# Transformer layers: the inverse roots of the query and key norms on another engine

## The chip, the cores and the metric

The kernel runs on one core of one Trainium2 chip. A core has five engines with a queue each: TensorE (PE in the profile), VectorE (DVE), ScalarE (ACT), GpSimd (POOL) and SyncE (SP), which issues most of the DMA transfers. The metric is the device time of one execution in microseconds, the median over the runs; lower is better.

## The reference

Two blocks run one after the other on x of shape (4, 512, 128). In the first, an attention that learns at test time is followed by a transformer of six layers. The second block has an attention with relative positions and a layer of experts. The change lies in the transformer of the first block. What matters of it, for each layer:

```python
def l2norm(t):
    return t / jnp.maximum(jnp.linalg.norm(t, axis=-1, keepdims=True), 1e-12)

def attn_layer(x, Wqkv, qs, ksc, Wo):
    ...
    q, k, v = (sh(q), sh(k), sh(v))          # 16 heads of 64
    q = l2norm(q) * qs
    k = l2norm(k) * ksc
    ...                                      # rotary, with cos, sin and a scale
    out = local_attention(q, k, v)           # windows of 32, each query sees its own and the one before
    return out.transpose(0, 2, 1, 3).reshape(b, n, INNER) @ Wo

for i in range(DEPTH):                       # 6 layers
    x = attn_layer(shift_tokens(x), Wqkv[i], q_scale[i], k_scale[i], Wo[i]) + x
    x = ffn_layer(shift_tokens(x), ln_g[i], ln_b[i], W1[i], b1[i], W2[i], b2[i]) + x
```

So each layer needs, for 4 batches, 512 tokens and 16 heads, the inverse root of a sum of 64 squares, once for queries and once for keys.

## The kernel before

The kernel has four phases with a meeting of all engines between them; the transformer is the second, from about 120 to 1850 us of the span. Its work is cut into 24 units, one for each layer and batch (unit u is layer u // 4, batch u % 4). A unit is laid over 110 steps ("rounds"), and a new unit starts every 32 steps, so up to four units overlap. No planner sorts the work: every engine walks through the same generator `rounds()` and issues, in each round, first the attention parts and then the units' steps that are due. Constants such as `NORM_AT` and `PART_AT` say at which step each piece of work is issued. A queue is in order, and the engines keep in step by semaphores alone; a `Signal` is one with named events.

The steps of one unit that matter here:

- Steps 0 to 31, eight times four steps: TensorE projects one group of four heads (lines 1109 to 1111, first four times keys, then four times queries), ScalarE squares it (line 1290), VectorE multiplies it with the rotary tables (line 1418, four instructions; it needs the tables' results of the group before to be merged), GpSimd adds the squares of the two halves (line 1552) and merges the rotated halves (lines 1558 and 1559). TensorE sums the squares over the head (line 1139), and VectorE collects the sums in `norms[kind]`, 128 x 128 numbers for one kind (lines 1427 and 1429; kind 0 is keys, kind 1 is queries). TensorE may project into a PSUM bank again only when VectorE has rotated what is in it.
- Step 17 ("root0", the key root) and step 33 ("root1", the query root): VectorE bounds `norms` from below (line 1434) and runs `inverse_root`, eleven instructions with a wait for the one before in front of each.
- The key roots then go through a DMA to memory and back, spread over partitions (lines 937 and 955), and VectorE multiplies the keys with them (line 1443). The query roots are transposed at step 39 (line 1143), copied by ScalarE (line 1295) and multiplied into the scores by VectorE (line 1485).

The attention of a unit is cut into eight parts of ten steps that start every four steps. For a part, TensorE computes scores (line 1208), VectorE scales them and takes the negated largest (lines 1485 and 1490), ScalarE takes exponentials with their sums (line 1354), VectorE inverts the sums (line 1493), GpSimd scales the exponentials (line 1573), TensorE transposes them (line 1216), ScalarE copies them (line 1360), TensorE weighs the values (line 1226), and after every second part mixes the heads (line 1234). The root steps fall one round before the round in which VectorE inverts the sums and GpSimd scales, of whichever part is due. The sync engine also issues the copies of the values into windows (lines 970 to 975), in the same order of rounds.

Of the kernel before, what the change touches and what calls it, by code (L numbers as in the profile page):

```python
# [10 lines left out]
I32 = mybir.dt.int32  # L11
ALU = mybir.AluOpType
# [4 lines left out]
P = 128  # L17
# [700 lines left out]
NORM_AT = {"root0": 17, "out": 15, "root1": 33, "turn": 39, "copy": 39}  # L718
# [67 lines left out]
def transformer_setup(c, t, scope):  # L786
# [8 lines left out]
    t.wide = [sb(f"rnorm_wide{i}", [P, S]) for i in range(2)]  # L795
    t.norms, t.rn, t.rn_t = [sb(f"norms{i}", [P, P]) for i in range(2)], [sb(f"rnorm{i}", [P, P]) for i in range(2)], t.wide[0][:, 0:P]
    t.rn_dram = [nc.dram_tensor(f"rnorms{i}", (32, S), F32, kind="Internal").ap() for i in range(2)]
    t.least, t.root_c = sb("least", [P, 1]), sb("root_constants", [P, 2], I32)
    t.rq = [sb(f"rnorm_tok{i}", [P, TPB, 32]) for i in range(2)]
    t.vt = [sb(f"v_tok{i}", [P, 2, PAIRS, DH]) for i in range(2)]  # L800
    t.v = [sb(f"v_win{i}", [P, TPB, PAIRS, DH]) for i in range(2)]
# [7 lines left out]
    one = lambda name, over: Signal(nc, "tf_" + name, over)  # L809
    pairs, halves = range(2 * GROUPS_TF), range(2)  # L810
    t.projected, t.squared, t.rotated = (per(n, units, [(p, h) for p in pairs for h in halves]) for n in ("projected", "squared", "rotated"))
    t.made, t.squares, t.summed, t.counted = (per(n, units, pairs) for n in ("made", "squares", "summed", "counted"))
    t.rooted, t.rn_turned, t.rn_kept = per("rooted", units, halves), one("rn_turned", units), one("rn_kept", units)
    t.rn_out = Signal(nc, "tf_rn_out", units, 16)
    t.wide_in = [Signal(nc, f"tf_wide_in{i}", [(u, g, j) for u in units for g in range(i, GROUPS_TF, 2) for j in range(4)], 16) for i in range(2)]
    t.k_scaled = per("k_scaled", units, range(GROUPS_TF))
# [584 lines left out]
def unit_vector(c, t, u, s):  # L1401
# [19 lines left out]
    if 0 <= p < 2 * GROUPS_TF and at == 0:  # L1421
        ps = ring_bank(c, t, "unit", u, f"sum{p}")[:, 0:P]
        kind, first = divmod(p, GROUPS_TF)
        V.wait_ge(*t.summed.on((u, p)))
        if first:
            V.wait_ge(*t.counted.on((u, p - 1)))
            V.e.tensor_tensor(t.norms[kind][:, :], t.norms[kind][:, :], ps, ALU.add).then_inc(*t.counted.by((u, p)))
        else:
            V.e.tensor_copy(t.norms[kind][:, :], ps).then_inc(*t.counted.by((u, p)))
    for kind in range(2):  # L1430
        if s == NORM_AT[f"root{kind}"]:
            x = t.norms[kind][:, :]
            V.wait_ge(*t.counted.on((u, GROUPS_TF * (kind + 1) - 1)))
            V.e.tensor_tensor(x, x, t.least[:, 0:1].to_broadcast([P, P]), ALU.max).then_inc(*own.up())
            if u:
                V.wait_ge(*(t.rn_turned if kind else t.rn_out).on(u - 1))
            inverse_root(c, t.rn[kind][:, :], x, t.rn_t, t.rooted.by((u, kind)), t.root_c)
    if s in SCALE_AT:
        g = SCALE_AT.index(s)
        k = t.k[u % 2][:, g, :, WIN:WIN + S]  # L1440
# [72 lines left out]
def transformer_pool(c, t):  # L1513
    G = c.G
    for high, low in t.xs:
        G.e.memset(high[:, :].bitcast(F32), 0.0)
        G.e.memset(low[:, :].bitcast(F32), 0.0)
    for k in t.k:
        G.e.memset(k[:, :, :, 0:WIN], 0.0)
    G.e.memset(t.v[0][:, 0, :, :], 0.0)  # L1520
    G.e.memset(t.xf[:, :], 0.0)
    G.e.memset(t.least[:, :], 1e-24)
    G.e.memset(t.root_c[:, 0:1], 1)
    G.e.memset(t.root_c[:, 1:2], 0x5F3759DF).then_inc(*t.zeroed.by(0))
    G.wait_ge(*t.normed.on(0))
    shift_gpsimd(c, t, 0)
    for now in rounds():
        for kind, n, s in now:
            if kind == "part":
                part_gpsimd(c, t, n, s)  # L1530
            elif kind == "unit":
                unit_gpsimd(c, t, n, s)
# [12 lines left out]
def unit_gpsimd(c, t, u, s):  # L1545
# [8 lines left out]
    if 0 <= p < 2 * GROUPS_TF and at == 0:  # L1554
        kind, g, lo = piece(p)
        G.wait_ge(*t.rotated.on((u, (p, 1))))
        first, second = made_of(t, u, kind, g)
        G.e.tensor_tensor(first, first, t.turned_by[0][:, :], ALU.subtract)
        G.e.tensor_tensor(second, second, t.turned_by[1][:, :], ALU.add).then_inc(*t.made.by((u, p)))  # L1559
    if b == B - 1 and l + 1 < DEPTH:  # L1560
        for x, (k, when) in enumerate(SPLIT_AT.items()):
            if s == when:
# [929 lines left out]
```

## Time and profile before

| | before |
|---|---|
| time, median of 2 runs | 2526.78 us (2521.78 and 2531.78) |
| span of the profiled execution | 2515.4 us |
| its TensorE clock, mean over the span | 0.971 of full speed |
| TensorE busy | 2362.9 us, 94% |
| VectorE busy | 1744.7 us, 69% |
| ScalarE busy | 1598.6 us, 64% |
| GpSimd busy | 1463.1 us, 58% |

The profile gives for the profiled execution its span, from the first to the last instruction, and no total time of its own; the times of the runs contain the span and what lies around it. A busy TensorE is not a TensorE at its peak, since the ends of its pipelined matmuls are modelled.

### The profile page before, as it was taken

The numbers are of one execution on the slowest core, as the hardware profiler recorded it, in microseconds if no ns is written. First come the engines' busy times: TensorE is split into PE (matmuls) and PEld (weight loads), VectorE is DVE, ScalarE is ACT, GpSimd is POOL, SyncE is SP. The second block draws the span as 40 slices with busy tenths as digits, with TensorE's granted clock in tenths as the row PEclk, the third lists the DMA queues.
The fourth block names the chain that finished last, engine by engine and source line by source line (L and its number), as shares of the span: only waits on it lengthen the run. The fifth ranks groups of instructions, "written<-read, shape, count | busy, mean of one in ns | idle before, by whom it ended". The sixth has DMA issues, their size and how long they took to land.

```text
span 2515.4 us, 122084 instructions
## 1 busy us (share of the span) xinstructions
PE 2362.9 (94%) x53677; PEld 1738.9 (69%) x53677; DVE 1744.7 (69%) x3537; ACT 1598.6 (64%) x5036; POOL 1463.1 (58%) x1408
## 2 busy tenths in 40 slices
PE   9958999999999999999999999999878999999967
PEld 8836777777777777777777777777645666666657
DVE  4477888888878888878787888887335555555534
ACT  3226777777777787777777877777625444545422
POOL 1166667656666667666666677665117656566307
PEclk9979999999999999999999999999979999999978
DMA  4013333333333334333333343333216222222136
GB/s 91 15 33 86 85 78 96 95 80 85 93 88 94 81 83 103 92 83 81 88 95 85 79 97 82 84 92 84 57 22 185 48 48 48 48 48 48 30 95 250
DMA packets 230210, 204.62 MB, mean 81 GB/s; under 512 B 133687, under 2 KB 155464, under 8 KB 229552
## 3 DMA queue, kind: packets, MB, share of 16 engines
q1 hardware_dynamic: 225296, 190.91, 30.6%
q8 instruction: 422, 6.91, 1.2%
q0 software_dynamic: 2208, 5.58, 0.6%
q14 instruction: 108, 0.88, 0.1%
q10 hardware_dynamic: 2176, 0.33, 0.1%
HBM read 86.05 MB, written 15.70 MB: 40 GB/s over the span
## 4 chain that ended last, share of the span: by engine, by line
PE 72%; DVE 17%; issue 4%; SPq 2%; ACT 2%; DMA 1%; POOL 1%; POOLq 0%; ACTq 0%; DVEq 0%
PE psum L1208 8%; PE psum L1226 6%; PE psum L1955 5%; PE psum L1234 5%; PE psum L1109 5%; PE psum L1934 5%; PE psum L1940 4%; PE psum L1111 4%; PE psum L1110 3%; DVE kT L1443 3%; PE psum L1989 3%; PE psum L1979 3%; DVE rotated L1418 3%; PE psum L1185 2%; PE psum L1216 2%
## 5 line engine op out<-in xcount | busy, mean ns | idle before, releaser
L1354 ACT ACTIVATE p<-p,stat 128x64 f32<-128x64 f32 x1536 | 512.5, 336 | 40.1 <-DVE stat L1490 38.0
L1573 POOL TENSOR_TENSOR p<-p,inverse 128x512 f32<-128x512 f32 x192 | 200.2, 1043 | 465.9 <-DVE inverse L1493 464.9
L1208 PE MATMUL psum<-kT,qT 32*32 32x64 f32 x24576 | 306.7, 223 | 30.3 <-issue 29.1
L2088 DVE TENSOR_REDUCE largest<-psum 128x1 f32<-128x512 f32 x256 | 165.0, 686 | 228.0 <-PE psum L1940 228.0
L1208 PEld LDWEIGHTS psum<-kT,qT 32*32 32x32 f32 x24576 | 264.0, 103 | 82.2 <-issue 81.1
L1354 ACT ACTIVATION_READ_ACCUMULATOR p<-p,stat 128x1 f32 x1536 | 288.6, 188 | 0.0
L1418 DVE SCALAR_TENSOR_TENSOR rotated<-psum,scales,rotary 128x512 f32<-128x512 f32 x384 | 271.1, 742 | 24.3 <-ACT sq L1290 24.2
L1552 POOL TENSOR_TENSOR sq<-sq 128x512 f32<-128x512 f32 x192 | 245.1, 1276 | 42.4 <-ACT sq L1290 42.1
L1290 ACT ACTIVATE sq<-psum 128x512 f32<-128x512 f32 x384 | 212.8, 581 | 63.3 <-PE psum L1139 45.9
L1226 PEld LDWEIGHTS psum<-pT,v_win 64*64 64x64 f32 x12288 | 197.3, 135 | 47.6 <-issue 40.6
L1109 PE MATMUL psum<-xs,wqkv_high 128*128 128x512 f32 x384 | 204.9, 534 | 24.3 <-DVE rotated L1418 24.3
L2010 ACT ACTIVATE w_by_key<-psum 128x512 f32<-128x512 f32 x128 | 76.4, 597 | 230.5 <-PE psum L1955 230.5
L1226 PE MATMUL psum<-pT,v_win 64*64 64x32 f32 x12288 | 218.6, 221 | 1.5 <-ACT pT L1360 1.5
L1234 PEld LDWEIGHTS psum<-oT,wo 128*128 128x128 f32 x1536 | 188.0, 196 | 37.0 <-issue 28.0
L1234 PE MATMUL psum<-oT,wo 128*128 128x128 f32 x1536 | 198.9, 283 | 7.5 <-issue 4.2
L1360 ACT ACTIVATE pT<-psum 128x512 f32<-128x512 f32 x192 | 114.3, 596 | 135.7 <-PE psum L1216 135.5
L1303 ACT ACTIVATE v_tok<-psum 128x512 f32<-128x512 f32 x192 | 113.8, 593 | 96.5 <-PE psum L1111 78.7
L2100 POOL TENSOR_TENSOR q_by_head<-q_heads,mask_head 64x256 fp32r<-64x256 f32 x252 | 156.8, 622 | 15.4
L1559 POOL TENSOR_TENSOR qT<-qT,rotated 128x512 f32<-128x512 f32 x96 | 165.7, 1726 | 0.0
L2056 ACT ACTIVATE weights<-psum,largest 128x512 f32<-128x512 f32 x256 | 161.3, 687 | 3.6 <-DVE largest L2088 3.6
L1443 DVE TENSOR_TENSOR kT<-kT,rnorm_wide 128x1024 f32<-128x1024 f32 x96 | 155.7, 1622 | 5.4 <-DMA rnorm_wide<-rnorms 5.3
L1111 PE MATMUL psum<-xs,wqkv_high 128*128 128x512 f32 x384 | 155.0, 404 | 0.0
(352 smaller groups left out, 5448.6 us busy)
## 6 DMA issues: line engine op xcount, KB each, us to landing
v_win<-v_tok SPq DMA_DIRECT2D x576, 128.0 KB
rnorm_wide<-rnorms SPq DMA_DIRECT2D x384, 64.0 KB
v_win<-v_tok SPq DMA_DIRECT2D x336, 64.0 KB
q_rows<-q_rows_all SPq DMA_DIRECT2D x32, 512.0 KB, 4.6
tile_weights<-expert_table SPq DMA_DIRECT2D x23, 512.0 KB, 6.1
wqkv<-L_ffn_Wqkv SPq DMA_DIRECT2D x96, 64.0 KB, 2.4
rel_values<-sq SPq DMA_DIRECT2D x60, 64.0 KB, 2.2
wo<-L_ffn_Wo SPq DMA_DIRECT2D x48, 64.0 KB
```

What stands on the lines that cost most here:

```text
L1109: PE.e.matmul(out, w[0], x[1], start=True, stop=False)
L1111: return PE.e.matmul(out, w[0], x[0], start=False, stop=True)
L1208: last = PE.e.matmul(psum[WIN * blk:WIN * (blk + 1), f, out], q[rows, g, half, tok:tok + WIN], k[rows, g, half, tok:tok + 2 * WIN], start= ...
L1226: last = PE.e.matmul(psum[to:to + DH, 2 + o, at:at + WIN], v[rows, blk, 2 * (2 * a + o) + h, :], t.pt[h][rows, 2 * a + o, blk * WIN:(blk + ...
L1234: last = PE.e.matmul(ps[:, 0:P], t.wo[:, e, :], t.ot[e % 2][:, e // 2, :], start=(e == 0), stop=(e == PAIRS - 1))
L1290: A.e.activation(t.sq[half][:, :], c.psum[:, 4 + half, :], ACT.Square).then_inc(*t.squared.by((u, (p, half))))
L1354: last = A.e.activation(p, p, ACT.Exp, bias=t.stat[:, h, 2 * g + f:2 * g + f + 1], accum_out=t.sum[:, h, g, f:f + 1])
L1418: last = V.e.scalar_tensor_tensor(out=rot[x], in0=psum[:, 4 + half, :], scalar=scale, in1=table, op0=ALU.mult, op1=ALU.mult)
L1443: V.e.tensor_tensor(k, k, t.wide[g % 2][:, :].unsqueeze(1).to_broadcast([P, 2, S]), ALU.mult).then_inc(*t.k_scaled.by((u, g)))
L1552: G.e.tensor_tensor(t.sq[0][:, :], t.sq[0][:, :], t.sq[1][:, :], ALU.add).then_inc(*t.squares.by((u, p)))
L1559: G.e.tensor_tensor(second, second, t.turned_by[1][:, :], ALU.add).then_inc(*t.made.by((u, p)))
L1573: G.e.tensor_tensor(p, p, t.inv[:, h, :, :].unsqueeze(3).to_broadcast([P, GROUPS_TF, 2, 2 * WIN]), ALU.mult).then_inc(*t.p_scaled.by(m))
```

## The change

VectorE keeps the bound of the norms at steps 17 and 33 (now signalled as `bounded`) and no longer calls `inverse_root` there. In the same rounds GpSimd waits for the bound and computes `norms ** -0.5` with one `tensor_tensor` of 128 x 128 against a column of -0.5. The wait that protects the old roots until they have been sent or transposed moves from VectorE to GpSimd, and VectorE waits before it overwrites `norms` until the power of the unit before has read it. `inverse_root` itself stays in use for the layer norms. Line numbers of the changed kernel differ by one to eight: the bound is line 1437 there, the power 1567, the scaling of the exponentials 1581.

```diff
-    t.rooted, t.rn_turned, t.rn_kept = per("rooted", units, halves), one("rn_turned", units), one("rn_kept", units)
+    t.bounded, t.rooted = per("bounded", units, halves), per("rooted", units, halves)
+    t.rn_turned, t.rn_kept = one("rn_turned", units), one("rn_kept", units)
...
         else:
+            if u:
+                V.wait_ge(*t.rooted.on((u - 1, kind)))
             V.e.tensor_copy(t.norms[kind][:, :], ps).then_inc(*t.counted.by((u, p)))
     for kind in range(2):
         if s == NORM_AT[f"root{kind}"]:
             x = t.norms[kind][:, :]
             V.wait_ge(*t.counted.on((u, GROUPS_TF * (kind + 1) - 1)))
-            V.e.tensor_tensor(x, x, t.least[:, 0:1].to_broadcast([P, P]), ALU.max).then_inc(*own.up())
-            if u:
-                V.wait_ge(*(t.rn_turned if kind else t.rn_out).on(u - 1))
-            inverse_root(c, t.rn[kind][:, :], x, t.rn_t, t.rooted.by((u, kind)), t.root_c)
+            V.e.tensor_tensor(x, x, t.least[:, 0:1].to_broadcast([P, P]), ALU.max).then_inc(*t.bounded.by((u, kind)))
...
     G.e.memset(t.least[:, :], 1e-24)
+    G.e.memset(t.power[:, :], -0.5).then_inc(*c.g_own.up())
...
+    G.wait_ge(*c.g_own.now())
     for now in rounds():
...
+    for kind in range(2):
+        if s == NORM_AT[f"root{kind}"]:
+            G.wait_ge(*t.bounded.on((u, kind)))
+            if u:
+                G.wait_ge(*(t.rn_turned if kind else t.rn_out).on(u - 1))
+            G.e.tensor_tensor(t.rn[kind][:, :], t.norms[kind][:, :], t.power[:, 0:1].to_broadcast([P, P]), ALU.pow).then_inc(*t.rooted.by((u, kind)))
```

What this does to VectorE's queue at the query root of the fourth unit. Before, the eleven instructions of the chain stand ahead of the reciprocal of the exponential sums (`rnorm_wide0` serves the chain as scratch):

```order
L217 TENSOR_TENSOR rnorm_wide0<-norms1,root_constants 128x128
L219 TENSOR_TENSOR rnorm1<-root_constants,rnorm_wide0 128x128
L222 TENSOR_TENSOR rnorm_wide0<-rnorm1 128x128
L224 SCALAR_TENSOR_TENSOR rnorm_wide0<-rnorm_wide0,norms1 128x128
L226 SCALAR_TENSOR_TENSOR rnorm1<-rnorm_wide0,rnorm1 128x128
L222 TENSOR_TENSOR rnorm_wide0<-rnorm1 128x128
L224 SCALAR_TENSOR_TENSOR rnorm_wide0<-rnorm_wide0,norms1 128x128
L226 SCALAR_TENSOR_TENSOR rnorm1<-rnorm_wide0,rnorm1 128x128
L222 TENSOR_TENSOR rnorm_wide0<-rnorm1 128x128
L224 SCALAR_TENSOR_TENSOR rnorm_wide0<-rnorm_wide0,norms1 128x128
L226 SCALAR_TENSOR_TENSOR rnorm1<-rnorm_wide0,rnorm1 128x128
L1493 RECIPROCAL inverse<-sum 128x8
```

Now the reciprocal follows the bound directly.

VectorE's queue at the same place in the changed kernel:

```order
L1428 TENSOR_TENSOR norms1<-norms1,psum 128x128
L1437 TENSOR_TENSOR norms1<-norms1,least 128x128
L1493 RECIPROCAL inverse<-sum 128x8
L1419 SCALAR_TENSOR_TENSOR kT0<-psum,scales,rotary 128x512
L1419 SCALAR_TENSOR_TENSOR rotated1<-psum,scales,rotary 128x512
```

Only the bound is left between the last sum of squares and the reciprocal.

GpSimd's queue around the same query root, before (`p0` is the tile of exponentials, `sq0` the squares, `kT0` and `qT1` the rotated keys and queries):

```order
L1558 TENSOR_TENSOR qT1<-qT1,rotated0 128x512
L1559 TENSOR_TENSOR qT1<-qT1,rotated1 128x512
L1565 TENSOR_TENSOR wqkv_low<-wqkv1,wqkv_high 128x512
L1573 TENSOR_TENSOR p0<-p0,inverse 128x512
L1552 TENSOR_TENSOR sq0<-sq0,sq1 128x512
L1558 TENSOR_TENSOR kT0<-kT0,rotated0 128x512
L1559 TENSOR_TENSOR kT0<-kT0,rotated1 128x512
```

Nothing of the roots stands here. The subtraction of line 1565 belongs to the splitting of the next layer's weights and is issued in every fourth unit only.

GpSimd's queue at the same place in the changed kernel:

```order
L1560 TENSOR_TENSOR qT1<-qT1,rotated0 128x512
L1561 TENSOR_TENSOR qT1<-qT1,rotated1 128x512
L1573 TENSOR_TENSOR wqkv_low<-wqkv1,wqkv_high 128x512
L1567 TENSOR_TENSOR rnorm1<-norms1,power 128x128
L1581 TENSOR_TENSOR p0<-p0,inverse 128x512
L1554 TENSOR_TENSOR sq0<-sq0,sq1 128x512
L1560 TENSOR_TENSOR kT0<-kT0,rotated0 128x512
L1561 TENSOR_TENSOR kT0<-kT0,rotated1 128x512
```

The power stands directly ahead of the scaling of the exponentials. At the key roots it stands at the same place, with queries in place of the keys behind it.

## Rows read from the trace of the kernel before

**Rows 1.** Busy time over the whole span, by engine: busy us, share, instructions.

```profile
PE 2362.9 (94%) x53677; PEld 1738.9 (69%) x53677; DVE 1744.7 (69%) x3537; ACT 1598.6 (64%) x5036; POOL 1463.1 (58%) x1408
```

**Rows 2.** Busy time by engine in the transformer's steady stretch, 300 to 1750 us.

```profile
core 0: us, PE busy (x) PEld busy (x) DVE busy (x) ACT busy (x) POOL busy (x), PEclk, DMA share, GB/s
300.00:1750.00 1450.00, 1411.83 (x38373) 1046.24 (x38371) 1180.73 (x2400) 1117.60 (x3875) 959.04 (x745) 1.00 0.36 88
```

**Rows 3.** List of waits: who waited for what, us in total, times, longest.

```profile
POOL p L1573 <- DVE inverse L1493: 464.9, 164, 9.4
...
PE psum L1109 <- DVE rotated L1418: 24.3, 7, 6.2
...
PE psum L1216 <- POOL p L1573: 14.5, 17, 3.1
```

**Rows 4.** Timeline of VectorE at a query root: start us, duration us, instruction.

```profile
1133.61 1.06 DVE L1434 TENSOR_TENSOR norms<-norms,least 128x128 f32<-128x128 f32 x1
...
1138.25 0.19 DVE L1493 RECIPROCAL inverse<-sum 128x8 f32<-128x8 f32 x1
```

**Rows 5.** Timeline of GpSimd at the same query root; in brackets idle time before.

```profile
1138.52 1.04 POOL L1573 TENSOR_TENSOR p<-p,inverse 128x512 f32<-128x512 f32 x1 [4.00 <-DVE inverse L1493]
```

**Rows 6.** Timeline of TensorE at the same query root.

```profile
1137.42 2.05 PE L1234 MATMUL psum<-oT,wo 128*128 128x128 f32 x16
1139.62 0.66 PE L1216 MATMUL psum<-ident,p 128*128 128x128 f32 x4
```

**Rows 7.** Timeline of TensorE at the query root of the next unit.

```profile
1209.53 0.66 PE L1216 MATMUL psum<-ident,p 128*128 128x128 f32 x4 [1.36 <-POOL p L1573]
```

**Rows 8.** Timeline of ScalarE at the first query root: its last exponential.

```profile
1134.86 0.19 ACT L1354 ACTIVATION_READ_ACCUMULATOR p<-p,stat 128x1 f32 x1
```

**Rows 9.** Timeline of VectorE at the key root that follows.

```profile
1168.50 0.29 DVE L1434 TENSOR_TENSOR norms<-norms,least 128x128 f32<-128x128 f32 x1
...
1172.37 0.20 DVE L1493 RECIPROCAL inverse<-sum 128x8 f32<-128x8 f32 x1
```

**Rows 10.** Timeline of GpSimd at that key root.

```profile
1172.64 1.04 POOL L1573 TENSOR_TENSOR p<-p,inverse 128x512 f32<-128x512 f32 x1 [4.20 <-DVE inverse L1493]
```

**Rows 11.** Timeline of TensorE at that key root.

```profile
1174.56 0.60 PE L1216 MATMUL psum<-ident,p 128*128 128x128 f32 x4
```

**Rows 12.** Groups by form on VectorE: count, busy us, mean ns, idle before.

```profile
L224 DVE SCALAR_TENSOR_TENSOR rnorm_wide<-rnorm_wide,norms 128x128 f32<-128x128 f32 x144 | 43.1, 299 | 4.9
L222 DVE TENSOR_TENSOR rnorm_wide<-rnorm 128x128 f32<-128x128 f32 x144 | 43.0, 299 | 4.9
L226 DVE SCALAR_TENSOR_TENSOR rnorm<-rnorm_wide,rnorm 128x128 f32<-128x128 f32 x144 | 42.1, 293 | 4.9
...
L217 DVE TENSOR_TENSOR rnorm_wide<-norms,root_constants 128x128 int32<-128x128 int32 x48 | 18.6, 387 | 4.9
...
L219 DVE TENSOR_TENSOR rnorm<-root_constants,rnorm_wide 128x128 int32<-128x128 int32 x48 | 14.0, 292 | 1.7
```

**Rows 13.** Timelines of VectorE and TensorE at the first unit's key root.

```profile
146.92 1.23 DVE L222 TENSOR_TENSOR rnorm_wide<-rnorm 128x128 f32<-128x128 f32 x1
...
152.13 0.80 PE L1109 MATMUL psum<-xs,wqkv_high 128*128 128x512 f32 x1 [6.20 <-DVE rotated L1418]
```

**Rows 14.** Groups by form on GpSimd: the two cheapest kinds on 128x128.

```profile
L1774 POOL TENSOR_TENSOR v_far<-v_near,v_ends 128x128 f32<-128x128 f32 x16 | 7.3, 494 | 0.2
...
L2159 POOL CAST keys<-keys_far 128x128 fp32r<-128x128 f32 x8 | 2.4, 300 | 0.0
```

**Rows 15.** Timeline of the sync engine at the key root of rows 9.

```profile
1176.51 0.59 SPq L937 DMA_DIRECT2D rnorms<-rnorm  x1
```

**Rows 16.** Timeline of VectorE: the feed-forward norm's root behind that key root.

```profile
1176.65 1.12 DVE L217 TENSOR_TENSOR root_t<-var,root_constants 128x4 int32<-128x4 int32 x1
```

**Rows 17.** The bound of the norms, all 48: duration ns, min/median/max.

```profile
L1434 DVE TENSOR_TENSOR norms<-norms,least x48: 291/1045/1208, 145.2 to 1753.5; 128x128 f32<-128x128 f32 x48
```

More of the change, by code:

```diff
@@ L797, in transformer_setup @@
     t.rn_dram = [nc.dram_tensor(f"rnorms{i}", (32, S), F32, kind="Internal").ap() for i in range(2)]
-    t.least, t.root_c = sb("least", [P, 1]), sb("root_constants", [P, 2], I32)
+    t.least, t.power, t.root_c = sb("least", [P, 1]), sb("power", [P, 1]), sb("root_constants", [P, 2], I32)
     t.rq = [sb(f"rnorm_tok{i}", [P, TPB, 32]) for i in range(2)]
```

## The prediction

> **What bounds the kernel now.** I began with the busy times of the whole span [rows 1] and then took the stretch in which the transformer layers run, 300 to 1750 us [rows 2]. There TensorE is busy 1412 of 1450 us at full clock, VectorE 1181, GpSimd 959. So TensorE sets the pace, and a faster VectorE is worth only what TensorE loses by waiting for it. The list of waits says how much that is [rows 3]: TensorE waits 24.3 us in 7 places for the rotated halves from VectorE, nearly all in the first units, before the pipeline is full, and 14.5 us in 17 places for GpSimd's scaled scores (line 1573). GpSimd in turn sits idle 465 us ahead of that same line, waiting for VectorE's reciprocal of the exponential sums. That last number is what the change touches: VectorE computes the reciprocal right behind the root chain, in program order.
>
> Then I looked at one query root (the second of each unit) and one key root (the first) as rows in time. At the query root VectorE bounds the norms at 1133.61 to 1134.67 and gives the reciprocal at 1138.25 [rows 4]. GpSimd has been idle for 4.00 us when its scaling of the scores starts at 1138.52 [rows 5]. TensorE's last matmul ahead of the transposes began its group at 1137.42 and runs 2.05 us, and the transposes start at 1139.62, just behind the scaling's end at 1139.56 [rows 6]: here TensorE waits for GpSimd, which waits for the root chain. The exponentials had been done since 1135.05 [rows 8]. At the key root the same steps are 1168.50, 1172.37 and 1172.64 [rows 9, 10], but the scaling ends at 1173.68 and the transposes start at 1174.56 [rows 11], so there is 0.9 us to spare. Another query root shows an idle TensorE of 1.36 us in front of the transposes [rows 7].
>
> **Part 1: eleven VectorE instructions go, 48 times.** From the groups by form [rows 12]: shift 387 ns, subtraction 292, three each of 299, 299 and 293 ns, so 0.39 + 0.29 + 3 x 0.89 = 3.35 us, with the small gaps between them 3.6 us each time, as the two samples also say (1134.67 to 1138.25). Over 24 units with two roots that is 173 us of VectorE. Nearly all of it lies beside a busy TensorE and is worth nothing by itself. What it can give back is the wait of rows 3: at most 14.5 us ahead of the transposes, and in the first unit the two chains, 2 x 3.6 = 7 us, of which the first (one of its instructions starts at 146.92) stands inside the 6.20 us that TensorE waits up to 152.13 [rows 13].
>
> **Part 2: one GpSimd power on 128x128 comes in, 48 times.** No row shows a power, so its duration X is bounded. From below by one pass over such a tile: 0.30 us for a cast and 0.49 us for a two-input operation [rows 14]; a power cannot cost less than nothing, since it is added work. Nearest to what it computes is the chain itself: eleven passes at these two rates are 3.3 and 5.4 us. A power needs a logarithm, a product and an exponential, more steps than eleven, but it need not write each step to SBUF. From above I take 25 such steps at the two-input rate, 25 x 0.49 = 12.3 us. My value is 4.9 us, in the upper half of the eleven-pass bracket, because the steps are more; both ends stay for the range.
>
> The Trainium skill, GPSIMD Engine Reference, section 7 (Performance pitfalls for Q7 kernels), says a chain of dependent fp32 steps costs 4 cycles per element unless it is unrolled; with the 1.2 GHz of its section 1 that would be an estimate of 0.43 us a step on 128 elements, 4.7 us for eleven and 10.7 us for 25. No row here shows it. By it alone the sum would lie anywhere between my case and the last rival.
>
> **Part 3: where the power stands.** GpSimd's queue is now: additions of the rotated halves, power, scaling of the scores, sum of squares. The power waits for VectorE's bound, which ends at 1134.67 and 1168.79; the scaling is queued behind the power. Before, the scaling started 3.85 us after the bound's end in both samples (1138.52 - 1134.67, 1172.64 - 1168.79). So the break-even is X = 3.8 us: a shorter power lets the scaling start earlier, a longer one delays it by X - 3.8, with the transposes, the sum of squares and the additions behind it. At the query root the delay is TensorE's stall at once; at the key root the first 0.9 us are free. Per unit: (X - 3.8) + (X - 4.7), where these are positive.
>
> **Part 4: who waits for the roots themselves.** The query root feeds a transpose six rounds later; the key root feeds a DMA. That DMA was issued at 1176.51, 4.1 us after the old chain's end, because the sync queue was still behind value-window transfers [rows 15]. So a key root may be as late as bound + 7.7 us before anything behind it moves. At X = 4.9 this costs nothing; above 7.7 the broadcast and the first key scaling slip too.
>
> **Part 5: the shared port.** The bound (two SBUF inputs) took between 291 and 1208 ns, median 1045 [rows 17], and at 1133.61 it ended 0.15 us after GpSimd's previous instruction did (1138.52 - 4.00 = 1134.52) [rows 4, 5]: VectorE's two-SBUF-input instructions wait for a running GpSimd instruction. With a long power that matters for the next such VectorE instructions. The next one is the first step of the feed-forward norm's root, at 1176.65 [rows 16], 7.9 us after the key root's bound, so at X = 4.9 nothing is added. The Trainium skill, SBUF - State Buffer, section "SBUF: two separate sides", calls this an exclusive lock for the whole instruction; by it, the trace agrees, and a power of over 8 us would also stop VectorE.
>
> **Sum.** The profiled execution has a span of 2515.4 us; the median of the two runs is 2526.8, so 11.4 us lie around it, which the change leaves alone. With X = 4.9: query roots 24 x 1.1 = 26 us, key roots 24 x 0.2 = 5 us, less the 7 us of the first unit (VectorE is the later one there, and GpSimd has slack). That is +24: a span of 2539 us and a time of **2550 us**, 0.9% up. A change below 2% either way (50 us) is about what this kernel's measurement can tell from none, so I call it no change.
>
> **Rivals.**
> *Short power (X below 3).* For it: the cheap casts of rows 14, and idle GpSimd (a third of the stretch). The scaling then starts up to 2 us earlier at key roots and right after the exponentials at query roots, the 14.5 us of waiting go and the 7 us of the first unit: 2526.8 - 22 = 2505 us. Twice this, if VectorE's relief also removes small waits that I cannot separate, is 2483. Over 2% faster would need more than all the waits of rows 3 together, so it is nearly excluded.
> *Long power (X from 5.5 to 9), slower than before.* The mechanism is GpSimd's queue in front of the scaling; the place is the 48 transposes. It decides from (X - 3.8) + (X - 4.7) = 2.4 us a unit on, which with the 7 us returned is the 2% bound: X = 5.45. At X = 7: 24 x (3.2 + 2.3) - 7 = +125, 2652 us. Against it: eleven passes end at 5.4. For it: a power is more than eleven steps.
> *Very long power (over 9).* At 12.3 us: 24 x (8.5 + 7.6) = +386, 2913 us, plus the late key norms and the port. TensorE's clock might then fall in the gaps.
> *The power does nothing for TensorE.* If X happens to lie between 3 and 4.4, the scaling starts when it did and only the first unit gains: 2520 to 2530 us. This is inside my case.
>
> **Chances.** X between 3 and 5.45, my case, 2515 to 2577 us: 0.36 (above, the 2% bound; below, the first unit's 7 us and a part of the query roots' wait). Short power: 0.20, of which 0.04 over 2% faster. Long power: 0.24. Very long: 0.20. The range leaves out the very long power: from 2490 to 2740 us, the upper end being X = 8.8 (24 x 9.1). The likeliest case's own range is 2515 to 2577. Faster 0.04, same 0.36 + 0.16 = 0.52, slower 0.44.
>
> **What will show it.** First the mean of the power's row on GpSimd: it decides the case. Then GpSimd's idle time ahead of the scaling at root places, which should vanish, and TensorE's wait for the scaled scores ahead of the transposes, now 14.5 us: near 45 in my case, near 0 with a short power, over 130 with a long one. VectorE's busy time should fall by about 160 us whatever happens. The prediction is wrong if X is off, if TensorE's stalls at one place are made up at another (a stall lets VectorE and ScalarE get ahead), or if VectorE was holding TensorE back in ways that the list of waits does not name.

## The result and the profile after

| | before | after |
|---|---|---|
| time, median of 2 runs each | 2526.78 us | 3437.03 us (3435.48 and 3438.59) |
| ratio | | 1.358 [1.353, 1.364] |
| span of the profiled execution | 2515.4 us | 3433.6 us |
| TensorE clock, mean of the span | 0.971 | 0.843 |

The forecast was 2550 us, in a range of 2490 to 2740. The kernel became 36% slower, above the range.

Busy times of the changed kernel over the whole span (answers to [rows 1]):

```profile
PE 2503.3 (73%) x53677; PEld 1836.8 (53%) x53677; DVE 1612.2 (47%) x3009; ACT 1608.9 (47%) x5036; POOL 2445.2 (71%) x1457
```

VectorE lost 132.5 us of work, GpSimd gained 982. TensorE has the same 53677 instructions and is busy 140 us longer with them. In the steady stretch (answers to [rows 2]) it is no longer the engine that never rests:

```profile
300.00:2600.00 2300.00, 1564.20 (x39136) 1155.44 (x39136) 1086.64 (x1968) 1149.88 (x3962) 1862.25 (x804) 0.82 0.23 56
```

GpSimd has most of the busy time of this stretch, 1862 of 2300 us, and the granted clock has gone from 1.00 to 0.82.

The power itself: first its group by line (the last column is the idle time in front of it), then all 48 of them with durations in ns, min/median/max:

```profile
L1567 POOL TENSOR_TENSOR rnorm<-norms,power 128x128 f32<-128x128 f32 x48 | 995.0, 20729 | 13.6 <-DVE norms L1437 13.6
```

```profile
L1567 POOL TENSOR_TENSOR rnorm<-norms,power x48: 20727/20728/20757, 146.4 to 2640.2; 128x128 f32<-128x128 f32 x48
```

X of the prediction is 20.73 us, not 4.9, and varies by 0.03 us.

The list of waits (answers to [rows 3]):

```profile
PE psum L1217 <- POOL p L1581: 759.5, 48, 18.2
...
POOL p L1581 <- DVE inverse L1493: 316.4, 129, 8.1
...
PE psum L1140 <- POOL sq L1554: 43.4, 4, 19.8
...
PE psum L1110 <- DVE rotated L1419: 13.3, 7, 2.6
```

TensorE's wait ahead of the transposes went from 14.5 to 759.5 us. Of its 48 places 46 are long ones, 14.8 to 18.2 us, one for each root from the second unit on; the other two are 1.6 and 3.2 us. The two roots of the first unit, when there is no attention part to transpose yet, show as waits of 19.8 and 18.9 us ahead of the sums of squares; they are most of the 43.4 us of that row. So each of the 48 roots has its one long stall. The 24.3 us of the first units for the rotated halves fell to 13.3.

One query root of the changed kernel as rows in time, GpSimd first (answers to [rows 5]):

```profile
1360.39 20.73 POOL L1567 TENSOR_TENSOR rnorm<-norms,power 128x128 f32<-128x128 f32 x1
1381.10 1.04 POOL L1581 TENSOR_TENSOR p<-p,inverse 128x512 f32<-128x512 f32 x1
```

TensorE at the same place (answers to [rows 6, 7]):

```profile
1362.17 2.05 PE L1235 MATMUL psum<-oT,wo 128*128 128x128 f32 x16
1382.19 1.11 PE L1217 MATMUL psum<-ident,p 128*128 128x128 f32 x4 [17.97 <-POOL p L1581]
1383.10 1.91 PE L1181 MATMUL psum<-sq,w 128*128 128x512 f32 x2
1384.03 1.42 PE L1110 MATMUL psum<-xs,wqkv_high 128*128 128x512 f32 x1
1385.24 0.63 PE L1111 MATMUL psum<-xs,wqkv_low 128*128 128x512 f32 x1
...
1389.62 0.39 PE L1111 MATMUL psum<-wqkv_high,xs 128*128 128x512 f32 x1
```

VectorE at the same place:

```profile
1365.81 0.68 DVE L1490 TENSOR_REDUCE stat<-p 128x8 f32<-128x512 f32 x1
1385.12 0.75 DVE L1463 SCALAR_TENSOR_TENSOR act<-psum,b1c,act 128x512 f32<-128x512 f32 x1 [18.63 <-PE psum L1181]
```

The scaling follows the power with no gap; the 4.00 us of idle GpSimd of [rows 5] are gone. TensorE ends what it has at 1364.22 and then stands for 17.97 us. VectorE's next input comes from TensorE, so it stands as well, for 18.63 us: the relieved engine waits, through TensorE, for the one that took its work. And when TensorE starts again its transposes take 1.11 us where they took 0.66 [rows 6]; a matmul of line 1111 takes 0.63 us where 4 us later it takes 0.39. Busy times of three stretches, ahead of this stall, behind it, and from 1388 on; the granted clock, 1.00 at full speed, is the first number behind the last bracket:

```profile
1355.00:1364.20 9.20, 9.20 (x234) 6.59 (x232) 6.24 (x10) 9.17 (x29) 8.96 (x5) 1.00 0.26 64
...
1382.20:1384.00 1.80, 1.80 (x6) 1.28 (x7) 0.00 (x0) 0.64 (x2) 1.80 (x2) 0.50 0.00 0
...
1388.00:1390.00 2.00, 2.00 (x33) 1.40 (x30) 0.61 (x2) 0.50 (x2) 1.04 (x1) 0.98 0.00 0
```

**The sum of the parts.** Waits ahead of the transposes +745 us, ahead of the sums of squares +40 (43.4, before 3.5), for the rotated halves -11, TensorE's busy time +140: +914 of the span's +918.

### The profile page after: what moved, and what is told of

It reads as the page before. It is cut to its first block, busy times and chain, and to the rows that moved or that the text cites. A ratio compares the mean times of both kernels' runs of the same rounds, so it can differ in the third digit from the quotient of the medians.

```text
span 3433.6 us, 121651 instructions
## 1 busy us (share of the span) xinstructions
PE 2503.3 (73%) x53677; PEld 1836.8 (53%) x53677; DVE 1612.2 (47%) x3009; ACT 1608.9 (47%) x5036; POOL 2445.2 (71%) x1457
## 4 chain that ended last, share of the span: by engine, by line
PE 54%; POOL 32%; DVE 8%; issue 3%; ACT 1%; SPq 1%; DMA 1%; another core or an unknown queue 0%; POOLq 0%; ACTq 0%; DVEq 0%
POOL rnorm L1567 29%; PE psum L1209 5%; PE psum L1227 4%; PE psum L1110 4%; PE psum L1963 4%; PE psum L1942 3%; PE psum L1111 3%; PE psum L1112 3%; PE psum L1217 3%; PE psum L1948 3%; PE psum L1235 2%; PE psum L1181 2%; DVE kT L1443 2%; PE psum L1997 2%; PE psum L1987 2%
## 5 line engine op out<-in xcount | busy, mean ns | idle before, releaser
L1567 POOL TENSOR_TENSOR rnorm<-norms,power 128x128 f32<-128x128 f32 x48 | 995.0, 20729 | 13.6 <-DVE norms L1437 13.6
L1217 PE MATMUL psum<-ident,p 128*128 128x128 f32 x768 | 140.3, 314 | 761.9 <-POOL p L1581 759.5
L1217 PEld LDWEIGHTS psum<-ident,p 128*128 128x128 f32 x768 | 104.8, 160 | 785.7 <-POOL p L1581 772.5
L1463 DVE SCALAR_TENSOR_TENSOR act<-psum,b1c,act 128x512 f32<-128x512 f32 (+1 forms) x72 | 53.8, 749 | 431.3 <-PE psum L1181 421.7
L1227 PEld LDWEIGHTS psum<-pT,v_win 64*64 64x64 f32 x12288 | 218.7, 147 | 54.4 <-issue 46.0
L1227 PE MATMUL psum<-pT,v_win 64*64 64x32 f32 x12288 | 240.4, 231 | 1.9 <-ACT pT L1361 1.8
L1110 PE MATMUL psum<-xs,wqkv_high 128*128 128x512 f32 x384 | 228.8, 596 | 13.3 <-DVE rotated L1419 13.3
```

The source lines that it names most:

```text
L1110: PE.e.matmul(out, w[0], x[1], start=True, stop=False)
L1217: last = PE.e.transpose(psum[:, 2, g * P:(g + 1) * P], t.p[h][:, g, :, :].rearrange("p f k -> p (f k)"), c.ident[:, :])
L1227: last = PE.e.matmul(psum[to:to + DH, 2 + o, at:at + WIN], v[rows, blk, 2 * (2 * a + o) + h, :], t.pt[h][rows, 2 * a + o, blk * WIN:(blk + ...
L1567: G.e.tensor_tensor(t.rn[kind][:, :], t.norms[kind][:, :], t.power[:, 0:1].to_broadcast([P, P]), ALU.pow).then_inc(*t.rooted.by((u, kind)))
```

## Experiments

Each ratio is to the kernel before, timed with it on one chip. The median of the kernel before was 2519.29 us beside the first four below, 2515.41 beside scratch, warm, late17_36 and late20_36, 2519.94 beside warm68, late17_34, late18_34 and ffn, and 2516.09 beside newton2 and cols32.

### What sets the price of a power (price)

The kernel before, with powers of constant data at the start of GpSimd's work, nine of them and one product.

```diff
+    for k, n in ((0, 1), (0, 4), (0, 16), (0, 32), (0, 64), (0, 128), (0, 256), (1, 128), (2, 128)):
+        G.e.tensor_tensor(t.py[:, 0:n], t.px[:, 0:n], t.pe[:, k:k + 1].to_broadcast([P, n]), ALU.pow)...
+    G.e.tensor_tensor(t.py[:, 0:P], t.px[:, 0:P], t.pe[:, 0:1].to_broadcast([P, P]), ALU.mult)...
```

Here `pe` holds the exponents -0.5, 1.0 and 2.0.

> The kernel before, with a list of prices on GpSimd ahead of the transformer's loop: powers of one constant tile of 3.7 with exponent -0.5 on 1, 4, 16, 32, 64, 128 and 256 columns, with exponents 1.0 and 2.0 on 128 columns, and one product on 128. In the changed kernel the power took 20.73 us on 128 columns in all 48 places. If the price is per element and does not depend on the data, it is 0.162 us a column: 0.2 us plus 0.65 at 4 columns, 5.2 at 32, 10.4 at 64, 41.4 at 256, and the same 20.7 us for all three exponents. If a good part is fixed (loading of code, a table), 1 and 4 columns come out at several us. If it depends on the values, the constant tile or the exponents 1 and 2 differ from 20.73 us by over 5%. The product takes 0.3 to 0.5 us.

GpSimd's groups by form in this kernel: count, busy us, mean ns, idle before.

```profile
L1530 POOL TENSOR_TENSOR price_out<-price_in,price_exponent 128x128 f32<-128x128 f32 x3 | 62.2, 20719 | 0.2
L1530 POOL TENSOR_TENSOR price_out<-price_in,price_exponent 128x256 f32<-128x256 f32 x1 | 41.1, 41115 | 0.1
...
L1530 POOL TENSOR_TENSOR price_out<-price_in,price_exponent 128x64 f32<-128x64 f32 x1 | 10.5, 10520 | 0.1
L1530 POOL TENSOR_TENSOR price_out<-price_in,price_exponent 128x32 f32<-128x32 f32 x1 | 5.4, 5414 | 0.1
...
L1530 POOL TENSOR_TENSOR price_out<-price_in,price_exponent 128x1 f32<-128x1 f32 x1 | 0.6, 587 | 0.1
...
L1532 POOL TENSOR_TENSOR price_out<-price_in,price_exponent 128x128 f32<-128x128 f32 x1 | 0.4, 398 | 0.1
```

From 32 to 256 columns it grows by (41115 - 5414) / 224 = 159 ns a column, with some 0.3 us besides. The three powers of 128x128 have the exponents -0.5, 1.0 and 2.0 and constant data, and take the same 20.72 us; in the layers, with real norms, it is 20.73. So neither the exponent, of the three tried, nor the data, a constant or real norms, sets it. The kernel with this list took 2638.23 us in its one run; in it TensorE waited 120.8 us in one piece at the start. The product of the same shape takes 0.40 us: one power is the price of 52 products.

### The same queue with a cheap operation (cheap)

```diff
-            G.e.tensor_tensor(t.rn[kind][:, :], t.norms[kind][:, :], ..., ALU.pow)...
+            G.e.tensor_tensor(t.rn[kind][:, :], t.norms[kind][:, :], ..., ALU.mult)...
```

The roots are replaced by a product; every wait stays.

> The changed kernel with a product in place of the power, so the roots are not computed; everything else, order and waits, as in the changed kernel. X falls from 20.73 to about 0.4 us. Queue theory (the loss is the power's own time in GpSimd's queue ahead of the scaling of the exponentials): all of the loss goes, TensorE's 14.5 us of waiting for the scaling and the first unit's 7 us go too, 2505 us (2495 to 2515). Rival, VectorE's relief is worth much more than the listed waits (its line stood in 17% of the chain): 2470 us or less. Rival, the new hand-over from VectorE to GpSimd costs something of itself: 2530 us or more.

Measured: 2492.25 us, ratio 0.989 [0.985, 0.993]. TensorE's waits:

```profile
PE psum L1110 <- DVE rotated L1419: 15.1, 7, 3.3
...
PE psum L1217 <- POOL p L1581: 6.0, 3, 3.2
```

The move alone, with its new waits between engines, costs nothing that shows and gives 27 us (17 to 39 by the interval of the ratio). Of these the list names 8.5 us at the transposes and 9.2 at the rotated halves. It is 3 us below the expected range, and no rival was met. The difference between this kernel and the changed one is the duration of 48 instructions, and it is 945 us.

### The power at a chosen length (cols24, cols32, cols40)

The power is taken of the first n columns only, and a product of the others, so that X can be set. The roots of the other columns are left out.

```diff
+            G.e.tensor_tensor(t.rn[kind][:, n:P], t.norms[kind][:, n:P], ..., ALU.mult)
+            G.e.tensor_tensor(t.rn[kind][:, 0:n], t.norms[kind][:, 0:n], ..., ALU.pow)...
```

> The changed kernel with a power on 24 of the 128 columns and a product on the other 104, so most roots are not computed. By 0.162 us a column X is 3.9 + 0.35 = 4.25 us. Queue theory, with the break-even of 3.8 us at the query root and 4.7 at the key root: 24 x 0.45 - 7 = +4, 2530 us (2515 to 2540). If VectorE's blocked two-input instructions or late roots made the loss in proportion to X: 910 x 4.25 / 20.73 = +187, 2713 us.

> The changed kernel with a power on 40 columns and a product on 88, so most roots are not computed. X is 6.5 + 0.35 = 6.85 us. Queue theory: 24 x (3.05 + 2.15) - 7 = +118, 2645 us. If TensorE's clock falls after stalls of 2 to 3 us as it did after those of 18 (0.82 in the stretch of the layers), some 50 us more: 2695. In proportion to X: 910 x 6.85 / 20.73 = +301, 2828 us.

> The changed kernel with a power on 32 columns and a product on 96, so most roots are not computed. By the price list X is 5.41 + 0.35 = 5.8 us. Waiting alone: 24 x (2.0 + 1.1) - 7 = +67, 2586 us. If stalls of 1 to 2 us already bring the clock down: TensorE's busy time, 2362 us at X = 4.5 and 2449 us at X = 7.1, lies well above 2362 and the time at 2610 to 2640 us. If the clock needs longer stalls: 2362 us busy and 2586 us.

X is the two instructions together (power 4.16, 5.43 and 6.75 us, product 0.36, 0.35 and 0.33). "Delay" is TensorE's wait at the transposes and at the sums of squares behind a root; "formula" is the prediction's 24 x [(X - 3.8) + (X - 4.7)], where positive, with the 18 us (14.5 + 3.5) that were there before.

| | X, us | time, us | ratio | delay, us | formula | PE busy, us | clock |
|---|---|---|---|---|---|---|---|
| before | | 2526.78 | | 18.0 | | 2362.9 | 0.971 |
| cheap | 0.40 | 2492.25 | 0.989 | 10.7 | | 2360.4 | 0.968 |
| cols24 | 4.52 | 2530.93 | 1.004 [1.003, 1.006] | 44.7 | 35 | 2362.2 | 0.969 |
| cols32 | 5.78 | 2596.55 | 1.033 [1.030, 1.035] | 92.1 | 91 | 2375.0 | 0.964 |
| cols40 | 7.09 | 2714.46 | 1.077 [1.073, 1.081] | 149.0 | 154 | 2448.6 | 0.934 |
| after | 20.73 | 3437.03 | 1.358 [1.353, 1.364] | 802.9 | 809 | 2503.3 | 0.843 |

The delay stays within 10 us of the formula from X = 4.5 to 20.7 us. cols24 is near the X that the prediction took: it is 11.6 us above the kernel before, and the prediction's own sum gives 24 x 0.72 - 7 = +10 at its X. The rival of a loss in proportion to X (2713 us for cols24, 2828 for cols40) is out. cols32 came out between its two cases (2586 by waiting alone, 2610 with the clock), and cols40 19 us above its case with the clock (2695). What the formula lacks is the column beside it: TensorE's own work grows, by 12 us where the longest stall at the transposes was 3.4 us (cols32), by 86 where it was 5.1 (cols40), by 140 where it was 18.2.

### Late roots or a blocked queue (scratch)

The chain goes back to VectorE and makes the roots; the power is computed at its place into a tile that nobody reads.

```diff
+            inverse_root(c, t.rn[kind][:, :], x, t.rn_t, t.rooted.by((u, kind)), t.root_c)
...
-            G.e.tensor_tensor(t.rn[kind][:, :], t.norms[kind][:, :], ..., ALU.pow).then_inc(*t.rooted...)
+            G.e.tensor_tensor(t.scrap[:, :], t.norms[kind][:, :], ..., ALU.pow).then_inc(*t.powered...)
```

> The changed kernel with the chain of eleven back on VectorE, whose roots are used by everyone, and the power kept at its place in GpSimd's queue but written to a tile that nobody reads. Queue theory: what costs is that GpSimd is taken for 20.7 us ahead of the scaling; nobody needs to wait for the roots. 3437 us, or a little more (up to 10 us) since the chain is back: 3430 to 3450. Rival, late roots (the sync queue waited 298 us for them, and the transposed query roots come 20 us later): half or more of the loss goes, under 3000 us.

Measured: 3433.03 us, ratio 1.365 [1.360, 1.369]; TensorE's first wait:

```profile
PE psum L1218 <- POOL p L1584: 759.0, 48, 18.3
```

The roots are early again and the time is that of the changed kernel, with the wait alike to 0.5 us. So what is queued behind the power on GpSimd makes the loss. That the roots come late costs nothing that can be seen; what it could cost at most is what the chain, now back, might cost again, some 27 us by cheap. In the changed kernel the sync engine did wait for a key root from 1421.2 to 1434.55, when the power ended, but VectorE waited for a transfer of the roots only once, for 0.8 us: all else was standing too.

### The clock (warm, warm68)

In both, TensorE multiplies an identity matrix into an unused stretch of PSUM ahead of the transposes of each root from the first attention part on (46 places), so that it is not idle in the stall.

```diff
     if s == PART_AT["turn"]:
+        if m % 8 in (2, 6) and m < 184:
+            for _ in range(68):        # 140 in warm
+                PE.e.matmul(psum[:, 3, 2 * P:3 * P], c.ident[:, :], c.ident[:, :], start=True, stop=True)
         PE.wait_ge(*t.p_scaled.on(m))
```

> The changed kernel with the whole power, and ahead of the 46 transposes that wait for it TensorE gets 140 more matmuls of 128x128 (0.11 us each by the transposes' own spacing, 15.4 us), into PSUM columns that nobody reads. They fit into the stall of 18 us. Clock theory: in the changed kernel TensorE is busy 140 us longer than before for the same matmuls because it comes out of each stall at the lower clock (0.82 granted in the layers); kept busy, it stays at full clock and the time falls by about 140 us, to 3300 us (3270 to 3330), though TensorE has 708 us more work. If the 140 us have another cause, the time stays at 3437 us or grows.

> The run with TensorE kept busy, repeated with a filling that fits. In the first one each of the 140 extra matmuls took 0.226 us (it stands in the trace as two records of 0.113 us), so a filling lasted 31.6 us and was 13.6 us longer than the stall. Now 68 of them, 15.4 us. Clock theory: 3437 less 104 to 140 us, so 3300 to 3335 us. The first run agrees roughly: 3959 - 46 x 13.6 = 3333. If the loss has no part that depends on the clock: 3437 us.

warm was a miss of its design: 140 such products are 31.6 us, longer than the stall that they were to fill, and it took 3959.09 us, ratio 1.574 [1.569, 1.579]. It says only that the clock was 0.975 when TensorE hardly stopped at the transposes (5.2 us in all). With 68 of them, 15.4 us, the time is 3316.53 us, ratio 1.316 [1.313, 1.319], 120 us below the changed kernel (106 by the two ratios, each to its own kernel before), though TensorE does more. Its group of fillers, each of them two records, and what it still waited for:

```profile
L1215 PE MATMUL psum<-ident 128*128 128x128 f32 x6256 | 707.2, 275 | 0.3 <-issue 0.3
```

```profile
PE psum L1220 <- POOL p L1584: 68.4, 40, 3.2
```

TensorE is busy 3094.8 us in all, 2387.6 without the fillers; in the changed kernel the same work took 2503.3. So 116 us of the 140 came from the idle time that the fillers took away, and the mean clock went from 0.843 to 0.961. Behind the stall of the rows above, TensorE ran at the lower of its two levels, 1.2 GHz (granted 0.50 from 1382.20 to 1384.00 and still from 1386 to 1388), and was back at 2.4 GHz (0.98) from 1388 to 1390; before the stall it had 1.00. The Trainium skill, TensorE: Matmul & The Clock Gate, Part 1 (The HAM clock gate), has the clock fall when the engine idles; by that, the trace agrees.

### Another cure: the chain where GpSimd does not wait for it (late17_36, late17_34, late18_34, late20_36)

Before, GpSimd idled 4 us behind the chain. These four kernels are the kernel before, with the chain on VectorE and only its step moved, away from the scaling.

```diff
-NORM_AT = {"root0": 17, "out": 15, "root1": 33, "turn": 39, "copy": 39}
+NORM_AT = {"root0": 17, "out": 15, "root1": 36, "turn": 39, "copy": 39}
```

The names give root0 and root1 in that order. The expectations are those of late17_36, late20_36, late17_34 and late18_34.

> The kernel before with one number changed: the query root's chain on VectorE is issued at step 36 instead of 33, behind the negated largest and so beside ScalarE's exponentials, no longer ahead of the reciprocal. The query roots have 9 us to spare before their transpose, so 3 rounds (6.5 us) later should hurt nobody. The 14.5 us of TensorE's waits ahead of the transposes are nearly all at query roots: 2519 - 12 = 2507 us (2500 to 2512). If the chain only moves the wait to the next reciprocal: 2519 us.

> As the run before, with the key root at step 20 instead of 17 as well. The key roots had 4.1 us to spare at the sync queue, and three rounds are 6.5 us, so the broadcast of the key norms comes 2 to 3 us later; the first key scaling may then wait for its transfer. If that wait lands on TensorE: 2507 + 24 x 2 = 2555 us; if it is hidden as the 5.3 us of such waits of before were: 2505 to 2515 us.

> The kernel before with the query root's chain at step 34 instead of 33: it then stands behind the reciprocal of the exponential sums and still ahead of the rotation, on VectorE. At step 36 it stood ahead of the feed-forward products, and TensorE waited 88 us for those. Here only the reciprocal and so GpSimd's scaling come 3.7 us earlier, nothing else moves. Queue theory: the 14.5 us of waits ahead of the transposes go, 2519 - 14 = 2505 us (2498 to 2512). If VectorE's rotation behind the chain is next in line: 2519 us.

> As the run before, and the key root's chain at step 18 instead of 17, behind the reciprocal and the rotation of its round. The key roots come some 3 us later and had 4.1 us to spare at the sync queue. If they are in time: 2505 us, or up to 5 us less; if the transfer is late: up to 2530 us.

| | time, us | ratio | wait at the transposes | the wait that grew (before) | PE busy |
|---|---|---|---|---|---|
| late17_34 | 2586.02 | 1.027 [1.024, 1.029] | 6.4 | rotated halves 50.3 (24.3) | 2387.3 |
| late17_36 | 2632.47 | 1.046 [1.043, 1.049] | 5.7 | activation, line 1463, 88.2 | 2407.3 |
| late18_34 | 2698.42 | 1.070 [1.068, 1.073] | 4.8 | `z`, line 1497, 92.7 | 2432.9 |
| late20_36 | 2737.33 | 1.089 [1.085, 1.092] | 10.7 | activation, line 1463, 84.9 | 2442.9 |

Each time the wait at the transposes falls, as it should, and each time the kernel is slower; all four expectations missed, the nearest by 67 us. The chain of 3.6 us holds whatever stands behind it on VectorE. In late17_36, VectorE's rows behind the chain, and TensorE's at that place:

```profile
1212.45 0.29 DVE L226 SCALAR_TENSOR_TENSOR rnorm<-rnorm_wide,rnorm 128x128 f32<-128x128 f32 x1
1212.66 0.74 DVE L1463 SCALAR_TENSOR_TENSOR act<-psum,b1c,act 128x512 f32<-128x512 f32 x1
```

```profile
1213.46 2.08 PE L1180 MATMUL psum<-sq,w 128*128 128x512 f32 x2 [4.11 <-DVE act L1463]
1214.55 1.42 PE L1109 MATMUL psum<-wqkv_low,xs 128*128 128x512 f32 x1
```

At step 33 the chain stood in front of a wait that TensorE hardly felt; at step 36 it stands in front of an activation that TensorE needs at once. It waits there 22 times, 4.11 us in this one, and slower matmuls stand behind (1.42 us here). For the other three the table names the wait, but their rows were not followed. So the step of the chain was no free choice, and the idle GpSimd of 4 us was not by itself a loss.

### A power where it is small, and a shorter chain (ffn, newton2)

ffn is the kernel before, with the feed-forward norm's root, 128 x 4 numbers, as a power on GpSimd.

```diff
-        inverse_root(c, c.rstd[:, b, :], c.var[:, b, :], c.root_t[:, 0:TPB], t.f_rooted.by(u), t.root_c)
...
+    if s == FFN_AT["root"]:
+        G.wait_ge(*t.f_varied.on(u))
+        G.e.tensor_tensor(c.rstd[:, b, :], c.var[:, b, :], t.power[:, 0:1].to_broadcast([P, TPB]), ALU.pow)...
```

> The kernel before, with the power where it is small: the feed-forward norm's root, 128x4, as one power on GpSimd (1.0 us by the price list) in place of the chain of eleven on VectorE (11 x 0.16, the first one 0.91 since it waits for GpSimd: 2.9 us with gaps). The power is waited for by nobody in a hurry: the spread comes 4 rounds later. Queue theory: 24 x 1.0 us on GpSimd, far from the scaling, costs nothing; VectorE gets 70 us back, worth 0 to 12 us: 2507 to 2519 us. If GpSimd's 1.0 us lands ahead of the scaling each time: 2519 us to 2530.

Measured: 2520.18 us, ratio 1.000 [0.998, 1.002]. That is a microsecond above the case in which nothing is gained. VectorE is busy 1696.4 us, 48 less, and nothing comes of it: TensorE waits 18.1 us at the transposes, 14.5 before.

newton2 leaves out the third Newton step of the key and query roots, so that the chain has eight instructions; the roots are less exact by that.

```diff
-            inverse_root(c, t.rn[kind][:, :], x, t.rn_t, t.rooted.by((u, kind)), t.root_c)
+            inverse_root(c, t.rn[kind][:, :], x, t.rn_t, t.rooted.by((u, kind)), t.root_c, steps=2)
```

> The kernel before with two Newton steps instead of three in the chains of the key and query norms (the layer norms keep three): eight VectorE instructions instead of eleven, so the reciprocal comes 3 x 0.33 = 1.0 us earlier at each root, at the place and with the neighbours that it has. Queue theory: of the 14.5 us of TensorE's waits ahead of the transposes some 12 go and 2 us in the first unit: 2519 - 14 = 2505 us (2500 to 2512). If taking the chain away pays only as a whole (the product in place of the power gave 27 us): 2519 us.

Measured: 2504.61 us, ratio 0.995 [0.993, 0.997], 11.5 us below the kernel before, as expected. It is the only version here that computes all roots, if less exactly, and is faster than the kernel before; the gain is clear of the noise and small. The wait at the transposes fell from 14.5 to 6.5 us. It takes from the chain what the change wanted gone, and puts nothing in another queue.

## Why the prediction was wrong, step by step

- **What bounds the kernel: right.** TensorE was the bound and VectorE's relief by itself worth little. ffn takes 48 us of VectorE away for nothing.
- **Part 1, the chain's removal: right.** The most it could give was 14.5 + 7 us; cheap gave 27 with a nearly free operation, 5 us more than the 22 of the short-power rival, which lies inside the interval of 17 to 39. Of the fall in VectorE's busy time, forecast at about 160 us, 132.5 came (159.2 in cheap). Of the 27 us between these two, 13.6 are one instruction, the first step of the feed-forward norm's root (24 times 747 ns here, 179 in cheap); Part 5 has why.
- **Part 2, X = 4.9 us: this step failed.** It measured 20.73 us. The bounds, 0.49 to 12.3, did not hold it either. The value came from the price of passes over the tile, eleven of them, and the upper end from 25, at the two-input rate of [rows 14]. No row of the trace showed an operation of that kind. The chain of eleven passes was the nearest row in what it computes and not in how it is run: a product on this engine costs 0.40 us at this shape, and the power 52 of them. The estimate from the Trainium skill's chain of dependent steps (GPSIMD Engine Reference, section 7; 4.7 us for eleven, 10.7 for 25) had the same fault, a count of steps that nothing here supported; at its 0.43 us a step, 20.73 us would be 48 of them. The honest reading of "no row shows it" was an upper end that the trace did not give, and a range that the forecast's 8 in 10 could not hold.
- **Part 3, the break-evens and the formula: right.** Delay against formula is 92.1 to 91, 149.0 to 154 and 802.9 to 809 us. With X = 20.73 the sum would have been 24 x (16.93 + 16.03) - 7 = +784, 3311 us; 3437 was measured, 126 more. The rival with a very long power had the mechanism and the place; its price ended at 12.3 us. (Its sum, +386, leaves out the 7 us that the others take off; it is +379.)
- **The clock: named and not priced.** "TensorE's clock might then fall in the gaps" was said of the very long case and stood in no sum. TensorE's busy time grew by 86 us at X = 7.1 and by 140 at 20.7, which covers the 126 us left to 3437; fillers took 116 of the 140 away. This share begins within the long case: at X = 7 the forecast's 2652 us stands beside 2714 measured at 7.09.
- **Part 4, late roots: right where it was used, too careful beyond.** Above 7.7 us "the broadcast and the first key scaling slip too" is true of the broadcast, and the scaling of the keys never waited over 0.8 us; scratch shows no loss by the lateness, within the some 27 us that the chain could hide.
- **Part 5, the port: the short wait is there, the long one is not.** After an ordinary instruction the trace bears the wait out. Line 217 at the feed-forward norm's root, VectorE first, then GpSimd:

```profile
1438.45 0.80 DVE L217 TENSOR_TENSOR root_t<-var,root_constants 128x4 int32<-128x4 int32 x1
```

```profile
1437.95 1.27 POOL L1561 TENSOR_TENSOR qT<-qT,rotated 128x512 f32<-128x512 f32 x1
```

  It ends at 1439.25, 0.03 us after the addition on GpSimd, and takes 0.80 us where its shortest takes 0.16. This was also the instruction that was to meet a long power. It did not: its input comes from TensorE, which stood still as well, so it started behind the power and not beside it, and all 24 took at most 803 ns. But scratch has what Part 5 asks for, the chain on VectorE beside a power that reads `norms` from SBUF. GpSimd, then VectorE at a query root, and all instructions of line 224 there:

```profile
1359.11 1.34 POOL L1576 TENSOR_TENSOR wqkv_low<-wqkv,wqkv_high 128x512 fp32r<-128x512 f32 x1
1360.40 20.78 POOL L1570 TENSOR_TENSOR scrap<-norms,power 128x128 f32<-128x128 f32 x1
```

```profile
1359.33 1.26 DVE L217 TENSOR_TENSOR rnorm_wide<-norms,root_constants 128x128 int32<-128x128 int32 x1
1360.62 0.37 DVE L219 TENSOR_TENSOR rnorm<-root_constants,rnorm_wide 128x128 int32<-128x128 int32 x1
...
1361.36 0.29 DVE L224 SCALAR_TENSOR_TENSOR rnorm_wide<-rnorm_wide,norms 128x128 f32<-128x128 f32 x1
...
L224 DVE SCALAR_TENSOR_TENSOR rnorm_wide<-rnorm_wide,norms x144: 291/293/294, 147.3 to 2653.5; 128x128 f32<-128x128 f32 x144
```

  The chain's first instruction waits for the ordinary subtraction (1.26 us, ending 0.14 behind it). The other ten then run beside the power, which lasts until 1381.18, and so do the ten others of all 48 chains: line 219 takes 0.37 us, 0.08 more than before, and the rest take 0.29 as before, with two inputs in SBUF as well. So a power of over 8 us does not stop VectorE, and this part of the prediction is refuted. The exclusive lock for the whole instruction, which Part 5 took from the Trainium skill (SBUF - State Buffer, section "SBUF: two separate sides"), does not describe the power; the measurement decides. Why the power differs from the additions stays open.
- **Signs to look for.** The power's row decided the case, as said; GpSimd's idle time ahead of the scaling vanished at root places; the wait at the transposes was over 130 us. That last sign was set too high for a part of its case: at X = 5.78, inside the "long" rival, cols32 waited 79.5 us there, and the prediction's own formula gives 88 (14.5 + 24 x 3.06). That a stall is made up elsewhere did not happen: the delay arrived whole (802.9 us of 809).

## What to carry to other kernels

An operation that no row of the trace shows has no price, however many rows stand for its parts: measure it alone, at two or three sizes, before it is put in a queue that feeds the busiest engine. Before an operation moves to an idle engine, look at what is queued behind it there; the idle 4 us was about the most that could stay free, and each further microsecond was paid by TensorE in full, 48 times, and at long stalls again in its clock. Where a dependent chain is in the way, shortening it, at the price of less exact roots, was worth more here than moving it to another engine or another step.

## What the runs showed of the hardware

- A power on GpSimd (f32, `tensor_tensor` with `pow`) takes 0.59 us at one column, 5.41 at 32, 20.72 at 128 and 41.1 at 256: 159 ns a column of 128 partitions, with exponents -0.5, 1.0 and 2.0 alike. A product takes 0.40 us at 128.
- An idle TensorE costs more than its idle time: 48 stalls of 14.8 to 19.8 us added 140 us to work that did not change, of which fillers gave 116 back. In cols32, with waits of up to 3.4 us at the transposes, it was 12.
- VectorE's instructions with two SBUF inputs did not wait for a running power: beside one of 20.8 us the 144 of line 224 took 291 to 294 ns (scratch). Behind an ordinary GpSimd instruction such a one was held, 0.80 us in place of 0.16 and 1.26 in place of 0.29.
